# A macaron transformer and state-space kernel: value mixing in pairs of chunks, the products by C moved to GpSimd, some copies moved to VectorE

## The reference, cut to what matters

```python
x = x + 0.5 * L0_ffn(ln(x))            # linear on inputs quantised to a 6-bit grid, blocks of 32
x = x + L0_attn(ln(x))                 # causal attention, one head of 128
x = x + 0.5 * L0_ffn(ln(x))
x = x + 0.5 * L1_ffn(ln(x), ...)       # 16-head attention with mixtures on values and outputs
x = x + L1_attn(ln(x), ...)            # state-space (Mamba) layer
x = x + 0.5 * L1_ffn(ln(x), ...)       # the 16-head attention again
```

```python
w, sel = top_k(x @ Ws, 2); mix_v = sigmoid(w) spread over sel          # (t, head, expert)
v = einsum('bthe,bted->bhtd', mix_v, x @ Wv)                           # value mixing
attn = softmax(q k^T / 8) @ v                                          # 16 heads, 512 x 512
res = einsum('bthe,bthd,efd->bthf', mask_o, attn, Wo).sum(heads)
```

```python
h = exp(dt * A) * h + (dt * x) * B_t
y_t = sum over states of h * C_t        # the products by C, then their sum
```

## Time and profile before

| | |
|---|---|
| median of three runs | 2648.18 us |
| the profiled execution | 2646.63 us |
| its span, first to last instruction | 2644.8 us |
| TensorE busy | 2476.0 us, 94% |
| VectorE busy | 2101.0 us, 79% |
| ScalarE busy | 1914.7 us, 72% |
| GpSimd busy | 738.6 us, 28% |
| mean granted TensorE clock | 0.984 of full |

### The profile page before, as it was taken

One profiled execution on the slowest core, in us unless ns is written; L12 is line 12 of the kernel. 1 busy time (PEld: TensorE's weight loads), 2 busy tenths in 40 slices (PEclk: granted clock), 3 DMA queues, 4 the chain that ended last, 5 costly groups with the idle time before them and its releaser, 6 DMA issues.

```text
span 2644.8 us, 50256 instructions
## 1 busy us (share of the span) xinstructions
PE 2476.0 (94%) x16925; PEld 1576.0 (60%) x16925; DVE 2101.0 (79%) x3154; ACT 1914.7 (72%) x4558; POOL 738.6 (28%) x564
## 2 busy tenths in 40 slices
PE   5599999999999899999889999999999999999998
PEld 3355665655656556565565656656565656666665
DVE  7588786989879789888986998789788878866553
ACT  3366767877788578867776877788687878877674
POOL 1000001452145126504440453155035315500000
PEclk9799999999999999999999999999999999999999
DMA  3413334553455435455444553455455345544424
GB/s 142 123 42 79 92 89 124 158 137 97 99 153 162 98 107 132 140 133 131 117 104 121 155 135 104 117 154 144 113 157 159 100 110 153 143 107 112 104 69 96
DMA packets 636714, 318.58 MB, mean 120 GB/s; under 512 B 419568, under 2 KB 545584, under 8 KB 636080
## 3 DMA queue, kind: packets, MB, share of 16 engines
q1 hardware_dynamic: 630416, 313.54, 45.2%
q10 hardware_dynamic: 6048, 1.84, 0.3%
HBM read 241.36 MB, written 82.31 MB: 122 GB/s over the span
## 4 chain that ended last, share of the span: by engine, by line
PE 56%; DVE 24%; issue 10%; POOL 3%; DMA 3%; ACT 2%; SPq 1%; ACTq 0%; DVEq 0%; POOLq 0%
PE ps L755 12%; PE ps L764 11%; PE ps L777 10%; DVE h_ring L1281 7%; PE ps L744 6%; PE ps L823 4%; DVE h_nmax L1102 4%; PE ps L838 3%; PE ps L844 2%; POOL h_ring L691 2%; DVE h_ring L1291 2%; DMA h_pv<-pv_d 1%; PE ps L796 1%; PE ps L829 1%; POOL h_wide_c L700 1%
## 5 line engine op out<-in xcount | busy, mean ns | idle before, releaser
L943 ACT ACTIVATE h_prob<-ps,h_nmax 128x512 f32<-128x512 f32 x1024 | 715.0, 700 | 106.4 <-DVE h_nmax L1102 104.8
L1102 DVE TENSOR_REDUCE h_nmax<-ps 128x2 f32<-128x1024 f32 x512 | 621.5, 1214 | 126.3 <-PE ps L755 124.8
L764 PE MATMUL ps<-ident,h_prob 128*128 128x128 f32 x4096 | 619.8, 277 | 23.5 <-ACT h_probT L1067 14.2
L764 PEld LDWEIGHTS ps<-ident,h_prob 128*128 128x128 f32 x4096 | 472.2, 141 | 190.0 <-issue 109.3
L755 PE MATMUL ps<-h_qk 64*128 64x512 f32 x2048 | 579.9, 643 | 0.1
L1067 ACT ACTIVATE h_probT<-ps 128x512 f32<-128x512 f32 x796 | 482.6, 606 | 93.7 <-PE ps L764 90.7
L700 POOL TENSOR_TENSOR h_wide_c<-h_wide_c,h_ring 128x512 f32<-128x512 f32 x240 | 332.4, 1385 | 647.6 <-DVE h_ring L1291 647.5
L777 PE MATMUL ps<-h_probT,h_v_sb 128*64 128x256 f32 x4096 | 499.9, 386 | 5.6 <-ACT h_vT L995 2.4
L777 PEld LDWEIGHTS ps<-h_probT,h_v_sb 128*64 128x64 f32 x4096 | 272.1, 137 | 311.3 <-issue 147.1
L1281 DVE TENSOR_TENSOR_SCAN h_ring<-h_ring 128x512 f32<-128x512 f32 x256 | 399.5, 1561 | 34.2 <-POOL h_ring L691 17.9
L691 POOL TENSOR_TENSOR h_ring<-h_m_xpad,h_m_b_rows 128x512 f32<-128x512 f32 x256 | 351.5, 1383 | 238.6 <-DVE h_m_xpad L1402 230.0
(11 more groups left out here) (224 smaller groups left out, 2715.7 us busy)
## 6 DMA issues: line engine op xcount, KB each, us to landing
h_mix_diag<-mix_blocks SPq DMA_DIRECT2D x128, 512.0 KB, 4.2
at_d<-h_att SPq DMA_DIRECT2D x128, 256.0 KB, 2.4
h_m_b_rows<-dbl_d SPq DMA_DIRECT2D x128, 256.0 KB, 4.3
h_m_c_rows<-dbl_d SPq DMA_DIRECT2D x128, 256.0 KB, 4.2
h_mo_diag<-mo_blocks SPq DMA_DIRECT2D x120, 256.0 KB, 3.3
h_att<-at_d SPq DMA_DIRECT2D x120, 256.0 KB, 3.7
pv_d<-h_pv SPq DMA_DIRECT2D x64, 256.0 KB, 2.9
h_pv<-pv_d SPq DMA_DIRECT2D x256, 64.0 KB, 3.4
```

What stands on the lines that cost most here:

```text
L764: ins = pe.transpose(ps[:, TB + v % 2, k * P:(k + 1) * P], prob[:, v % NB, k * P:(k + 1) * P], ident[:, :])
L943: act.activation(prob[:, v % NB, :], ps[:, SB + v % 4, :], ACT.Exp, bias=nmax[:, p, j, o:o + 1], accum_out=den[:, p, j, o:o + 1]).then_inc ...
L1102: dve.tensor_reduce(nmax[:, p, j, :], ps[:, SB + 2 * w % 4:SB + 2 * w % 4 + 2, :], X, ALU.max, negate=True).then_inc(sem("row_max"), 1)
```

## The change

1. Products by C: `read` moves from VectorE's program to GpSimd's. GpSimd now multiplies and then adds, and does so for all 32 parts.
2. `by_act`: while the recurrence runs, VectorE copies every fourth turned block (units with v % 4 == 0), ScalarE the other three. Elsewhere nothing changes.
3. Value mixing stands first in its step beside P.V; the tie goes by name, so P.V is first and mixing follows. Six of the eight chunks of a job now fall in pairs into steps that have a P.V (offsets 58, 62, 66), one stands at 55, and the last at 70 behind a P.V.
4. Offsets in the table: turned values of the first two head pairs at 8 and 9 (before 4 and 8), the last at 54 (55), the output product at 51 (50), the second `top2` at 48 (44), and some others by one or a few steps.
5. `START` is 5 steps earlier against the first preparation, so the first job's units begin while its value mixing still runs.

```diff
-        START = FIRST_PREP + 51
+        START = FIRST_PREP + 46
...
-            "post": [((18, 22, 26, 30, 32, 38, 42, 46)[c], "omix", c) for c in range(NCO)] + [(50, "out", 0)],
+            "post": [((18, 22, 26, 30, 32, 38, 42, 46)[c], "omix", c) for c in range(NCO)] + [(51, "out", 0)],
...
-            + [((56, 57, 58, 61, 63, 64, 66, 67)[c], "vmix", c) for c in range(NCV)],
-            "first_prep": [((46, 47, 48, 49, 50, 51, 52, 53)[c], "vmix", c) for c in range(NCV)],
+            + [((55, 58, 58, 62, 62, 66, 66, 70)[c], "vmix", c) for c in range(NCV)],
+            "first_prep": [((47, 48, 49, 50, 51, 52, 53, 54)[c], "vmix", c) for c in range(NCV)],
...
-        FIRST_IN_STEP = {"att": 0, "omix": 1, "vmix": 1}
+        FIRST_IN_STEP = {"vmix": 0, "att": 0, "omix": 1}
...
-        TOP_AT = (AT["gate", 1] + 3, 44)
+        TOP_AT = (AT["gate", 1] + 3, 48)
...
-            return v % 2 == 1 or mamba_on(START + v)
+            return v % 4 != 0 if mamba_on(START + v) else v % 2 == 1
...
+                    def read(b, v):
+
+                        n, h = divmod(v, HALVES)
+                        w = b * UN + v
+                        pool.wait_ge(sem(f"c_in{n % 2}"), 16 * (NS // 2 * b + n // 2 + 1))
+                        pool.wait_ge(sem("state"), w + 1)
+                        place = mb["scan"][:, w % NSC, :]
+                        pool.tensor_tensor(mb["y"][:, h, :] if n == 0 else place, place, mb["c_rows"][:, n % 2, :],
+                                           ALU.mult).then_inc(sem("read"), 1)
...
-                                for v in range(HALVES, UN):
+                                for v in range(UN):
                                     if u == SCAN_AT[v] + 1:
-                                        add(n, v)
+                                        read(n, v)
+                                        if v >= HALVES:
+                                            add(n, v)
...
-                                for v_ in range(UN):
-                                    if u == SCAN_AT[v_] + 1:
-                                        read(n, v_)
```

More of the change, by code:

```diff
@@ L235, in macaron_kernel @@
             "heads": [(4 * a + 10, "att", a) for a in range(HALF)] + [(8 * p + 17, "back", p) for p in range(PAIRS)]
-            + [((4, 8, 15, 23, 31, 39, 47, 55)[p], "vturn", p) for p in range(PAIRS)] + [(8 * p - 5, "pq", p) for p in range(PAIRS)] + [(8 * p - 4, "pk", p) for p in range(PAIRS)],
-            "post": [((18, 22, 26, 30, 32, 38, 42, 46)[c], "omix", c) for c in range(NCO)] + [(50, "out", 0)],
+            + [((8, 9, 15, 23, 31, 39, 47, 54)[p], "vturn", p) for p in range(PAIRS)] + [(8 * p - 5, "pq", p) for p in range(PAIRS)] + [(8 * p - 4, "pk", p) for p in range(PAIRS)],
+            "post": [((18, 22, 26, 30, 32, 38, 42, 46)[c], "omix", c) for c in range(NCO)] + [(51, "out", 0)],
             "last": [((18, 22, 26, 30, 34, 38, 42, 46)[c], "omix", c) for c in range(NCO)]
@@ L240, in macaron_kernel @@
             "prep": [(10, "norm", 0), (13, "gate", 0), (16, "gate", 1)]
-            + [((21, 23, 26, 31)[j], "value", j) for j in range(J)]
-            + [((56, 57, 58, 61, 63, 64, 66, 67)[c], "vmix", c) for c in range(NCV)],
-            "first_prep": [((46, 47, 48, 49, 50, 51, 52, 53)[c], "vmix", c) for c in range(NCV)],
-            "front": [(15, "f_z", 0), (19, "f_lin", 0), (27, "f_norm", 0), (28, "f_key", 0), (32, "f_val", 0)]
-            + [((29, 31, 33, 35)[j], "f_score", j) for j in range(J)] + [((37, 38, 39, 44)[j], "f_turn", j) for j in range(J)]
+            + [((21, 23, 26, 30)[j], "value", j) for j in range(J)]
+            + [((55, 58, 58, 62, 62, 66, 66, 70)[c], "vmix", c) for c in range(NCV)],
+            "first_prep": [((47, 48, 49, 50, 51, 52, 53, 54)[c], "vmix", c) for c in range(NCV)],
+            "front": [(18, "f_z", 0), (19, "f_lin", 0), (27, "f_norm", 0), (28, "f_key", 0), (32, "f_val", 0)]
+            + [((29, 31, 33, 35)[j], "f_score", j) for j in range(J)] + [((36, 38, 39, 44)[j], "f_turn", j) for j in range(J)]
             + [(46, "f_att", 0), (60, "f_z", 1), (62, "f_lin", 1)],
@@ L1282, in scan @@
                                                ALU.mult, ALU.add).then_inc(sem("state"), 1)
-                    def read(b, v):
-                        n, h = divmod(v, HALVES)
-                        w = b * UN + v
-                        dve.wait_ge(sem(f"c_in{n % 2}"), 16 * (NS // 2 * b + n // 2 + 1))
-                        dve.wait_ge(sem("state"), w + 1)
-                        place = mb["scan"][:, w % NSC, :]
-                        dve.tensor_tensor(mb["y"][:, h, :] if n == 0 else place, place, mb["c_rows"][:, n % 2, :],
-                                          ALU.mult).then_inc(sem("read"), 1)
                     def gate_y(n):
```

## The result

The changed kernel takes 2664.42 us, the median of four runs (2659.55 to 2665.61), against 2648.05 (2647.19 to 2648.7, four runs as well) of the kernel before, run beside it: a ratio of 1.0059, with a 95% interval of 1.0041 to 1.0076. The forecast was 2614, range 2566 to 2652. The profiled execution took 2664.3 us with a span of 2662.5 and a mean granted clock of 0.979 (0.984 before).

The account below looks back on a forecast made before the run. TensorE was taken as the bound, with gaps mostly from waits on VectorE. Terms -6 - 11 + 0 - 15 - 6 - 8 + 12 = -34 us from 2646.6 gave 2612.6, 2614 as median, range 2566 to 2652.

Parts of the forecast that it names:

- What bounds the kernel: Whole run: TensorE is the bound; its waits lead mostly to VectorE, ScalarE being late through VectorE's row maxima.
- Start: First mixing: scores and turned blocks moved ahead hide in its load waits; -6 us, between nothing and 12 us won.
- Mixing next to P.V: TensorE, attention jobs: fewer changes between whole-array and half-column work; -11 us, bounds -8 and -15.
- Loads of pairs: Mixing's loads, two chunks issued together three steps ahead: taken as 0; +20 us if waits came in each job.
- Output product: TensorE's wait for VectorE to empty the bank of `back`: -15 us of 21.1, bounds -5 and -21.
- clock: TensorE's granted clock, lower after idling before the output product: -6 us, bounds 0 and -12.
- VectorE and GpSimd in the recurrence: Recurrence: products by C leave VectorE, copies come, port holds return most of the relief; -8 us, bounds -45 and +30.
- Copies on VectorE: Turned blocks in the recurrence: VectorE's copies may be at most 0.9 us late; +12 us, above 36, below nothing.
- The copies come late: Rival on VectorE's copies of turned blocks: all 36 us paid, with idle time and half clock; +2, 2650 us; chance 0.11.
- GpSimd becomes the bound: Rival in the recurrence: held GpSimd instructions make scans wait for `drive`, +59 us; +21 in all, 2669 us; chance 0.15.
- VectorE was the cause of nearly all of it: Rival on TensorE's waits: both large ones lead to VectorE, half of 89 us idle goes; -74, 2574 us; chance 0.24.
- The slower case: Outcome slower than before by over 0.2%, chance 0.15, which rested on GpSimd becoming the bound in the recurrence (2669 us).

Follow-up runs that it names:

- T: The kernel before with all changes of the table (order in a step, offsets, earlier start) alone, products and copies as before: 2612.5 us, ratio 0.9863.
- C: The kernel before with only the new rule that VectorE copies every fourth turned block while a recurrence runs: 2686.6 us, ratio 1.0145.
- T + C: The kernel before with the new table and VectorE's copies of every fourth unit, products by C still on VectorE: 2659.9 us, ratio 1.0045.
- R: The kernel before with only the products by C moved from VectorE to GpSimd: 2671.2 us, ratio 1.0084.
- T + R: The changed kernel with the old rule for copies, so new table and products by C on GpSimd: 2621.9 us, ratio 0.9901.
- outtop: The kernel before with only the output product at offset 51 instead of 50 and the second top2 at 48 instead of 44: 2624.1 us, ratio 0.9913.

## Why the prediction was wrong, step by step

- **What bounds the kernel**: right in the main. In T, C, T + C and the changed kernel TensorE's largest waits are for VectorE; in R and T + R its largest is for ScalarE's copies (24.8 and 22.0 us from 457 to 2330, before 13.8, T 11.7). That these are late through VectorE's row maxima was argued, not tested.
- **Start, -6**: -4.5 alone. The first P.V came 7.3 us earlier, not 6.
- **Mixing next to P.V, -11**: -16 alone, just beyond the bounds -8 and -15, which its interval (-11 to -21) takes in. The mechanism holds: 10.9 us of it are TensorE's own work. The other 6 us are idle time that went, which was not in the term. The pairs come out as predicted, as here in the changed kernel's 15th job, where the earlier trace rows had one chunk behind P.V:

```profile
2486.96 1.95 PE L789 MATMUL ps<-h_probT,h_v_sb 128*64 128x256 f32 x16
2488.73 1.90 PE L835 MATMUL ps<-h_mix_diag,h_pv 128*64 128x256 f32 x16
```

- **Loads of pairs, 0**: right. Mixing's whole idle time in the changed kernel is 7.1 us, of which 5.6 are waits for DMAs (15.7 and 11.7 before); the +20 was far off.
- **Output product, -15, and clock, -6**: right, -23 together; idle time in front of L856 is 2.8 us. In the changed kernel the clock's part is lost again: the mean is 0.979, where it was 0.984 before and 0.988 in `outtop`, with the new idle time.
- **VectorE and GpSimd in the recurrence, -8**: this step failed. It is +10 on T (6 to 10), +22 on the kernel before, and +4, not clear of noise, where C stands too. The errors are these. The hold was too small in sum and in the wrong place: the step gave 2.4 + 2.5 = 4.9 us for 14 parts, 0.35 us each, where T and T + R show 0.50. Its half for the scan (0.17 us each) was too large, the scan grew by 0.06; "some 25 other two-operand instructions held 0.1 us longer" was a guess, and three of them and a one-input instruction in one stretch are held by 0.8 to 1.0 us each. One-input instructions, 36 of the 129 us, were not in it at all. And the step took VectorE's busy time for time of the kernel: VectorE waited 39 us more for scores, so much of the relief fell where TensorE was the bound, while holds fell into stretches without air. The longer chain of GpSimd behind a scan, with `drive` at its end, stood in a rival and not in this term.
- **Copies on VectorE, +12**: this step failed most. It costs 38 to 48 us. The mechanism was the one described (0.9 us of room behind such a copy), but the upper bound, 142 copies late by a quarter of a us, had no row behind it: in the changed kernel the wait is 1.7 us in the mean where there is one (74.0 us in 44 waits up to 1650 us), and 95.4 us in all against 8.9 before, 0.6 us for each of the 142. The row that spoke against +12 was read beside it: in the full stretch VectorE waits 0.6 us in 14 row maxima, that is, it is never early there, so a copy in its list is late by whatever its list is late, and not by a quarter of a us. The copies of the earlier trace rows that wait for TensorE stand in jobs without a recurrence; they say nothing of one with it.
- **Sum**: -38 for the table, which measured -36; the other two terms +4 predicted, +52 measured. That -38 and -36 lie so close is in part luck: measured one by one the parts are -4.5, -16 and -23, and in T some of it is lost again.
- **The rivals**: "The copies come late" is what happened. Its sign was over 30 us of L776 behind L1345; the page has 95.4. Its price was right for the copies (36 us) but kept the -8 of the recurrence, and so ended at 2650. "GpSimd becomes the bound" did not happen: GpSimd's means are 1.31 to 1.43 us, under the 1.71 from which it would decide, scans wait 21.7 us in all for `drive` (the sign was 50), and it is busy 1063 us as forecast. The scan's mean is 1577 ns, just under the 1.6 to 1.8 forecast. "VectorE was the cause of nearly all of it" fell in this form with R, which took 51 us off VectorE's busy time on the kernel before (2101.0 to 2050.1 us) and 63 on T, and won nothing. The slower case should have carried the copies' lateness, not GpSimd's load.

## What to carry to other kernels

Before an engine that is late by design takes over the emptying of a bank, count the room between the instruction and who needs the bank, and compare it with how late that engine's list already runs in that stretch; an engine's share over the run says nothing about it. Work moved from VectorE to GpSimd is paid back in part by the instructions that stay behind, some with one input among them: here two thirds of it, and partly in stretches that could least afford it. Measure the parts of a combined change apart: here the table alone was worth 36 us, and the two moves put on top of it cost 52.
